# A convolution, attention and gated FFN kernel: t1 kept without its channel mean, and one power for two tiles

## The reference

```
x = inv(I - circulant(ricker(width, damp))) @ x        # over channels
t = tokens(x)
t = t + attention(ln(t))          # 8 heads of 16; linear: elu(q)+1, elu(k)+1, causal sums, divided by the sum of weights; then W_out
u = ln(t)                         # called z in the kernel
g = mean over positions of (relu(u @ gfc1.T + b) @ gfc2.T + b)     # 8 gates for each batch
W1m, b1m, W2m, b2m = base weights + sum over 8 experts of g * expert weights   # for each batch
res = u + relu(u @ W1m.T + b1m) @ W2m.T + b2m
out = t + ln(res) * gain + bias
```

## Time and profile before

| | |
|---|---|
| median of three runs | 734.12 us |
| the profiled execution | 735.35 us |
| its span, first to last instruction | 733.4 us |
| TensorE busy (weight loads, which overlap) | 683.1 us (531.0) |
| DVE, ACT, POOL busy | 647.6, 634.2, 498.8 us |
| first phase | from 16.5 us, steady from about 43 to 448 us, drained at 479.6 us |
| second phase | 479.9 to 733.4 us |

### The profile page before, as it was taken

The page is one execution under the profiler, slowest core; times in us unless marked ns, Lnnn a source line. Parts: engine busy times, 40 slices in busy tenths (PEclk is TensorE's granted clock), DMA queues, the critical chain, the costliest instruction groups (busy, mean ns, idle before and its releaser), DMA issues. The chain is left out here.

```text
span 733.4 us, 39983 instructions
## 1 busy us (share of the span) xinstructions
PE 683.1 (93%) x13026; PEld 531.0 (72%) x13026; DVE 647.6 (88%) x2535; ACT 634.2 (86%) x1780; POOL 498.8 (68%) x911
## 2 busy tenths in 40 slices
PE   3898999999999999999999998889999998999993
PEld 2576777777777777777777776767777797777772
DVE  5689999999999999999999999667998977998983
ACT  3689999999999999999999998457888876888883
POOL 3669999999999999999999997301333312333333
PEclk9999999999999999999999999799999999999998
DMA  4547876666666666666666665210222211222222
GB/s 138 109 111 130 154 139 151 143 147 147 148 138 156 143 144 149 147 152 144 143 149 151 136 142 119 38 37 17 77 83 72 86 44 45 87 72 72 86 86 72
DMA packets 200294, 82.58 MB, mean 113 GB/s; under 512 B 174028, under 2 KB 187503, under 8 KB 200184
## 3 DMA queue, kind: packets, MB, share of 16 engines
q1 hardware_dynamic: 200248, 81.98, 47.7%
HBM read 22.69 MB, written 17.30 MB: 55 GB/s over the span
## 5 line engine op out<-in xcount | busy, mean ns | idle before, releaser
L900 DVE SCALAR_TENSOR_TENSOR scores_lo<-p_a,scores_hi 128x512 f16<-128x512 f32 x256 | 170.6, 677 | 1.2 <-ACT scores_hi L781 1.2
L781 ACT ACTIVATE scores_hi<-p_a 128x512 f16<-128x512 f32 x256 | 162.7, 646 | 4.9 <-PE p_a L617 4.8
L1433 POOL TENSOR_TENSOR ffn_rstd_shift<-ffn_rstd_shift,consts 128x4 f32<-128x4 f32 x32 | 36.8, 1150 | 110.9 <-DVE ffn_rstd_shift L1391 110.9
L1260 ACT ACTIVATE h_f<-psb,merged_b_of_batch 128x512 f32<-128x512 f32 x128 | 87.3, 712 | 11.7 <-PE psb L1196 10.1
L1215 PE MATMUL psb<-merged_W_of_batch,h_hi 128*128 128x128 f16 x512 | 94.5, 220 | 2.3 <-DVE h_lo L1369 1.6
L1369 DVE TENSOR_TENSOR h_lo<-h_f,h_hi 128x512 f16<-128x512 f32 x128 | 95.5, 785 | 1.3 <-ACT h_hi L1271 1.2
L1216 PE MATMUL psb<-merged_W_of_batch,h_hi 128*128 128x128 f16 x512 | 94.2, 220 | 0.0
L1217 PE MATMUL psb<-merged_W_of_batch,h_lo 128*128 128x128 f16 x512 | 94.2, 220 | 0.0
L634 PE MATMUL p_o<-v_parts,scores_hi 128*128 128x17 f16 x1024 | 90.4, 171 | 2.4 <-issue 0.6
L1001 POOL CAST qk_parts<-qk_f 128x512 f16<-128x512 f32 x128 | 78.3, 612 | 17.9 <-issue 15.7
L634 PEld LDWEIGHTS p_o<-v_parts,scores_hi 128*128 128x128 f16 x1024 | 81.6, 96 | 11.8 <-issue 9.2
(11 more groups left out here) (214 smaller groups left out, 2775.3 us busy)
## 6 DMA issues: line engine op xcount, KB each, us to landing
x_f<-in_x SPq DMA_DIRECT2D x32, 256.0 KB, 3.0
t_rows<-t SPq DMA_DIRECT2D x64, 128.0 KB, 2.0
t_back<-t_rows SPq DMA_DIRECT2D x32, 256.0 KB, 2.6
out<-out_tile SPq DMA_DIRECT2D x32, 256.0 KB, 2.0
tv_share<-in_L_ffn_tv_W SPq DMA_DIRECT2D x32, 128.0 KB, 2.2
qkT_parts<-qk_parts SPq DMA_TRANSPOSE x128, 3.1
zT_hi_lo<-z_parts SPq DMA_TRANSPOSE x64, 2.4
merged_W<-in_L_ffn_W SPq DMA_DIRECT2D x2, 256.0 KB, 4.3
```

What stands on the lines that cost most here:

```text
L781: nc.scalar.activation(ah[:, t % 2, cols], p_a[:, cols], ACT.Relu).then_inc(ahi_ready[eo], 1)
L900: nc.vector.scalar_tensor_tensor(al[:, t % 2, cols], p_a[:, cols], 0.0, ah[:, t % 2, cols], ALU.max, ALU.subtract).then_inc(alo_ready[eo], 1)
L1260: nc.scalar.activation(hf_[:, c, :], ps[:, c, :], ACT.Relu, bias=b1s[:, h // 2, c:c + 1], scale=1.0 / WS).then_inc(h_ready[c], 1)
```

## The change

t1 is made without its mean over channels. The inverse's part of `out_project` is now taken from the centred inverse, W_out is centred too, and a column with the mean is put beside them, so that the matmuls have 129 columns; the setup makes these columns. `yt`, its rows in DRAM and `t1_back` are 129 wide. z then needs no bias: `shift2` is gone, and `normalise` is a copy with a scale. `eps2` and `rsqrt2` handle two tiles at once, at the second of them; for this z and all behind it (`normalise`, `z_hi`, `z_lo`, `turn_z`, `gate`, `gate_relu`) stand two slots later, and `stats2` has eight buffers in place of four. In the second phase a new operation on POOL, `add_mean`, adds the mean back to the loaded t1, and `add_up` waits for it in place of the load.

```diff
+C1 = C + 1
+Q0 = C + 16
-TENSOR_ORDER = [("gate", 14), ...
+TENSOR_ORDER = [("gate", 16), ...
-SCALAR_ORDER = [("v_hi", 2), ("normalise", 10), ...
+SCALAR_ORDER = [("v_hi", 2), ("normalise", 12), ...
...
-FFN_GPSIMD_ORDER = [("rsqrt", 2), ("gain", 2)]
+FFN_GPSIMD_ORDER = [("add_mean", 2), ("rsqrt", 2), ("gain", 2)]
...
-                    nc.vector.tensor_scalar(wbig[:, 0:C], pa[:, 1, 0:128], WSI, None, ALU.mult)
+                    nc.vector.tensor_scalar(wbig[:, 0:C], pa[:, 1, 128:256], WSI, None, ALU.mult)
+                    link(nc.vector.tensor_reduce(wom[:, 2:3], pa[:, 1, 0:128], AX.X, ALU.add))
+                    nc.vector.tensor_scalar(wbig[:, C:Q0], wom[:, 2:3].broadcast_to([P, Q0 - C]), WSI / C, None, ALU.mult)
                     link(nc.vector.tensor_copy(gfh[:, :], wsqT[:, 4, :]))
                     dve.wait_ge(s_wtc, 1)
-                    nc.vector.tensor_scalar(woT[:, :], wsqT[:, 3, :], WSI, None, ALU.mult)
+                    link(nc.vector.tensor_reduce(wom[:, 0:1], wsqT[:, 3, :], AX.X, ALU.add))
+                    link(nc.vector.tensor_scalar(wom[:, 1:2], wom[:, 0:1], 1.0 / C, None, ALU.mult))
+                    nc.vector.tensor_scalar(woT[:, 0:C], wsqT[:, 3, :], wom[:, 1:2], WSI, ALU.subtract, ALU.mult)
+                    nc.vector.tensor_scalar(woT[:, C:C1], wom[:, 1:2], WSI, None, ALU.mult)
...
-                        o, cols = p_m1[:, 0:P], slice(j * P, (j + 1) * P)
-                        mm(o, xh[:, hf, cols], wh[:, 0:C], start=True, stop=False)
+                        o, cols = p_m1[:, 0:C1], slice(j * P, (j + 1) * P)
+                        mm(o, xh[:, hf, cols], wh[:, 0:C1], start=True, stop=False)
...
-                        nc.scalar.activation(yt[:, t, :], p_m1[:, 0:P], ACT.Copy, scale=1.0 / WSI).then_inc(t1_ready, 1)
+                        nc.scalar.activation(yt[:, t, :], p_m1[:, 0:C1], ACT.Copy, scale=1.0 / WSI).then_inc(t1_ready, 1)
...
                     def normalise(b, t):
                         n = TILES * b + t
-                        act.wait_ge(shift_ready, n + 1)
+                        act.wait_ge(rstd2, n + 1)
                         at_least(act, zlo_ready, n - 1)
-                        nc.scalar.activation(z_[:, t % 2, :], yt[:, t, :], ACT.Identity, bias=st2[:, t % 4, 10:11],
-                                             scale=st2[:, t % 4, 8:9]).then_inc(z_ready, 1)
+                        nc.scalar.activation(z_[:, t % 2, :], yt[:, t, 0:C], ACT.Copy, scale=st2[:, t, 8:9])\
+                            .then_inc(z_ready, 1)
...
                     def eps2(b, t):
+                        if t % 2 == 0:
+                            return
                         n = TILES * b + t
                         dve.wait_ge(mv2, n + 1)
-                        nc.vector.tensor_scalar(st2[:, t % 4, 9:10], st2[:, t % 4, 7:8], EPS, None, ALU.add)\
-                            .then_inc(ve2, 1)
+                        nc.vector.tensor_scalar(st2[:, t - 1:t + 1, 9:10], st2[:, t - 1:t + 1, 7:8], EPS, None, ALU.add)\
+                            .then_inc(ve2, 2)
...
-                    def shift2(b, t):
-                        n = TILES * b + t
-                        dve.wait_ge(rstd2, n + 1)
-                        nc.vector.tensor_scalar(st2[:, t % 4, 10:11], st2[:, t % 4, 6:7], -1.0, st2[:, t % 4, 8:9],
-                                                ALU.mult, ALU.mult).then_inc(shift_ready, 1)
...
                     def rsqrt2(b, t):
-                        n = TILES * b + t
-                        s = st2[:, t % 4, :]
+                        if t % 2 == 0:
+                            return
+                        n = TILES * b + t
                         pool.wait_ge(ve2, n + 1)
-                        nc.gpsimd.tensor_tensor(s[:, 8:9], s[:, 9:10], mhalf, ALU.pow).then_inc(rstd2, 1)
+                        nc.gpsimd.tensor_tensor(st2[:, t - 1:t + 1, 8:9], st2[:, t - 1:t + 1, 9:10],
+                                                kcol("mhalf")[:, 0:2].unsqueeze(2), ALU.pow).then_inc(rstd2, 2)
...
-                        dve.wait_ge(t1_loaded[hf], 16 * (2 * pair + h // 2 + 1))
-                        nc.vector.tensor_tensor(rn[:, hf, :, :], rn[:, hf, :, :], t1b[:, hf, :, :], ALU.add)\
+                        dve.wait_ge(raised, q + 1)
+                        nc.vector.tensor_tensor(rn[:, hf, :, :], rn[:, hf, :, :], t1b[:, hf, :, 0:C], ALU.add)\
                             .then_inc(v_ready, 1)
...
+                    def add_mean(g, pair, h):
+                        q, hf = HB * pair + h, h % 2
+                        pool.wait_ge(t1_loaded[hf], 16 * (2 * pair + h // 2 + 1))
+                        nc.gpsimd.tensor_tensor(t1b[:, hf, :, 0:C], t1b[:, hf, :, 0:C],
+                                                t1b[:, hf, :, C:C1].broadcast_to([P, HALF, C]), ALU.add)\
+                            .then_inc(raised, 1)
```

More of the change, by code:

```diff
@@ L39 @@
 BIG = -1.0e30
-TENSOR_ORDER = [("gate", 14), ("project", 1), ("state", 3), ("scores", 4), ("turn_out", 6), ("conv", 0),
+TENSOR_ORDER = [("gate", 16), ("project", 1), ("state", 3), ("scores", 4), ("turn_out", 6), ("conv", 0),
                 ("values", 5), ("out_project", 6)]
-SCALAR_ORDER = [("v_hi", 2), ("normalise", 10), ("split_x", 0), ("tv_hi", 0), ("relu_qk", 2), ("gate_relu", 14),
+SCALAR_ORDER = [("v_hi", 2), ("normalise", 12), ("split_x", 0), ("tv_hi", 0), ("relu_qk", 2), ("gate_relu", 16),
                 ("read_t1", 7), ("exp_qk", 1), ("state_hi", 3), ("scores_hi_0", 4), ("copy_out", 6),
@@ L48 @@
 VECTOR_ORDER = [("invert", 6), ("stats2", 8), ("divide", 6), ("make_qk", 2), ("v_lo", 2), ("mean_var2", 8),
-                ("state_lo", 3), ("stats1", 0), ("tv_lo", 0), ("eps2", 8), ("shift2", 9), ("mean_var1", 0),
-                ("scores_lo_0", 4), ("eps1", 0), ("scores_lo_1", 4)]
-GPSIMD_ORDER = [("split_x", 0), ("rsqrt2", 9), ("qk_hi", 2), ("z_hi", 10), ("qk_lo", 2), ("z_lo", 10),
+                ("state_lo", 3), ("stats1", 0), ("tv_lo", 0), ("eps2", 8), ("mean_var1", 0), ("scores_lo_0", 4),
+                ("eps1", 0), ("scores_lo_1", 4)]
+GPSIMD_ORDER = [("split_x", 0), ("rsqrt2", 9), ("qk_hi", 2), ("z_hi", 12), ("qk_lo", 2), ("z_lo", 12),
                 ("rsqrt1", 0)]
-SYNC_ORDER = [("turn_z", 12), ("store", 7), ("turn", 2), ("load_x", 3), ("load_tv", 1)]
+SYNC_ORDER = [("turn_z", 14), ("store", 7), ("turn", 2), ("load_x", 3), ("load_tv", 1)]
 FFN_TENSOR_ORDER = [("up_0", 0), ("up_3", 0), ("up_1", 0), ("down_0", 1), ("down_1", 1), ("down_2", 1),
@@ L215, in build @@
             casd = sb(su, "cas_scaled", [P, 2, C])
-            wbig = sb(su, "w_in", [P, 4 * C])
+            wbig = sb(su, "w_in", [P, Q0 + 3 * C])
+            wom = sb(su, "w_out_mean", [P, 3])
             cw = sb(su, "centred_inverse", [P, C])
@@ L965, in _ @@
                     run(dve, VECTOR_ORDER, {"tv_lo": tv_lo, "stats1": stats1, "mean_var1": mean_var1, "v_lo": v_lo,
-                        "make_qk": make_qk, "shift2": shift2, "state_lo": state_lo,
+                        "make_qk": make_qk, "state_lo": state_lo,
                         "scores_lo_0": scores_lo(0), "scores_lo_1": scores_lo(1),
```

46 lines of the change are left out of this document (23 added, 23 removed).

## The result

The changed kernel takes 761.52 us (median of 6 runs, 759.41 to 762.92), the one before 734.63 in the same series: a ratio of 1.0359, 95% interval 1.0332 to 1.0387. The forecast was 766 with a range of 746 to 775, and slower with a chance of 0.84. The profiled execution has a span of 759.13 in place of 733.44.

| stretch | before | after | difference | predicted |
|---|---|---|---|---|
| start to the first `scores_lo` (setup) | 28.73 | 29.64 | +0.91 | +1.0 |
| to the end of the last `scores_lo` (first phase) | 431.28 | 427.63 | -3.65 | -2.2 |
| to the end of the last gate (drain) | 18.88 | 21.63 | +2.75 | +2.6 |
| to the first `gain` | 28.18 | 28.78 | +0.60 | 0 |
| to the end of the last `gain` (second phase) | 221.29 | 246.34 | +25.05 | +30.2 |

The account below looks back on a forecast made before the run. The second phase was taken as bound by a gain-to-gain loop without slack, the first by a four-tile loop across engines; 734.12 + 31.6 (+30.2 second phase, -2.2 first, +2.6 drain, +1.0 setup) gave 766, range 746 to 775.

Parts of the forecast that it names:

- add_mean on the two hidden_lo: Second phase: add_mean runs between the two hidden_lo and makes the second 1.08 later, 28 times, +30.2 us.
- rival 4: Second phase: add_mean waits for one hidden_lo and is slower than gain, giving 776 us; chance 0.06.
- That the loop has no slack and POOL's own time is free: Second phase: gain to gain fills the whole 6.55 period; POOL idles 2.3, so by its time alone add_mean costs nothing.
- Turns alternate: Second phase: DVE and POOL take turns by who waited longer, so add_mean gets in after the first hidden_lo.
- rival 1: Second phase: DVE keeps its turn, add_mean starts after add_up and the power is 0.55 later; 751 us, chance 0.14.
- Casts: Second phase: the cast beside POOL's power was not held up, so nothing was charged for casts.
- First phase: Four-tile loop: +0.20 for the power, -0.09 for normalise, -0.18 for DVE, so -0.07; 32 loops, -2.2 us.
- The pair's power: First phase: rsqrt2 making two columns takes 0.75 for 0.55, +0.20 on the four-tile loop.
- Drain and setup: End of first phase: last z two slots later, +2.6 us; setup: added row sums and small operations on DVE, +1.0.

Follow-up runs that it names:

- no_add: The changed kernel without POOL's add_mean, add_up waiting for the load itself; 733.31 us, ratio 1.0015 to the kernel before.
- power_in_place: The changed kernel with add_mean replaced, at the same place in POOL's queue, by a power of 128x4; ratio 1.0009 to the kernel before.
- early_before: The kernel before the change with mean_var and add_eps of the second phase moved right behind stats on DVE; 724.71 us, ratio 0.9904.
- after_power: The changed kernel with add_mean between the power and gain in POOL's order; 758.03 us, ratio 1.0335 to the kernel before.
- early_after: The changed kernel with mean_var and add_eps right behind stats on DVE and add_mean behind the power on POOL; ratio 0.9939 to the kernel before.
- bias_back: The changed kernel with the first phase's normalise reading a bias column again; ratio 1.0417 to the kernel before.
- two_powers: The changed kernel with the second norm's epsilon and power made for each tile separately, z still two tiles later; ratio 1.0346 to the kernel before.

## Why the prediction was right, point by point

- *add_mean on the two hidden_lo.* Right in mechanism and in order: POOL gets its turn between the two, the first is unchanged, the second waits and then runs its usual 0.55 past the end of the POOL operation. The mis-sized term is add_mean's duration: "the nearest row is `gain` with the same shape, 1.27". It takes 1.04. With that the step gives itself: 1.04 - 0.14 is 0.90, and add_mean ends 0.90 after the first `hidden_lo` (569.88 and 568.98). 1.08 - 0.23 is the measured 0.85, and 28 x 0.85 = 23.8 stands for 30.2. My rival 4, which made add_mean dearer than `gain`, erred to the other side.
- *That the loop has no slack and POOL's own time is free.* Shown by no_add and power_in_place. TensorE was nearer to being a bound than I wrote: with the stall gone the period falls only from 6.59 to 6.38 (early_before), so the loop was 0.21 longer than TensorE's own work.
- *Turns alternate* (against rival 1). That POOL gets in between two DVE operations that follow each other closely is shown by the two records above: had DVE kept its turn, the second `hidden_lo` would have stayed at 0.68 and add_mean's record been 2.9. Whether turns alternate, or simply go to the one that asked first, is not told apart: add_mean starts to wait at 568.39, the second `hidden_lo` at 568.90, and in after_power too the one that was 0.06 ahead went first.
- *Casts.* I charged nothing, since the cast beside the power was not held up. The number came out right, because no cast lies beside add_mean in the changed kernel; that is luck, for the reason was wrong and the row misread. The cast had begun first (563.27, the power at 563.42), so it was the power that had to wait, and it did: it took 1.15, where it takes 1.01 with nothing of DVE beside it (kernel before, near its end). Where the cast begins 0.06 ahead of it, it takes 1.23 (569.98, kernel before), and where the cast begins 0.21 behind it, 1.01 (646.86, changed kernel).

```profile
718.89 1.01 POOL L1433 TENSOR_TENSOR ffn_rstd_shift<-ffn_rstd_shift,consts 128x4 f32<-128x4 f32 x1 [2.32 <-DVE ffn_rstd_shift L1391]
```

  In early_after a cast beside add_mean takes 1.09 for 0.43, and power_in_place shows that a power of four columns does not hold up a `hidden_lo`. The Trainium skill (SBUF — State Buffer, section "Who interferes with whom") counts casts that run in a two-port mode among what contends with GpSimd; early_after agrees.
- *First phase.* The loop over four tiles with one normalise in it is confirmed to the hundredth by bias_back (-0.09). The pair's power was sized +0.20; two_powers shows its net as +0.09 with the halved epsilon in it. Part of the miss is the row I scaled from: the 1.15 of four columns has 0.14 of waiting for the cast in it; from 1.01 it is 0.15 per further column, and two columns take 0.70 (measured 0.71). What is left I put down to the loss of `shift2`, which no run tried by itself: 26.83 - 0.18 - 26.44 = 0.21 per eight tiles, 0.10 per loop, where I had -0.18 for DVE with both. Together -0.105 per loop and not -0.07. The stretch from first to last `scores_lo` differs by up to 3.7 us between profiles of kernels with the same first phase (426.11 to 429.85 in six of them), so the -3.65 of this pair is told less sharply than the period.
- *Drain and setup.* +2.75 and +0.91 where +2.6 and +1.0 stood. The drain with z at 12 took 19.44 to 21.63 in eight profiles, with z at 10 or 11 17.38 to 18.88 in six, so that a hit within 0.15 is partly luck. That TensorE's clock would be low behind it was not foreseen: 0.60 in this pair of profiles, 1.5 to 2.2 against those in which the clock of the kernel before does not fall.

## What to carry to other kernels

When POOL has idle time, ask what DVE does in it before giving it work: here a POOL operation on 512 elements per partition in SBUF held up each DVE operation with two inputs in SBUF that came while it ran, down to one of four elements per partition, and a cast of 128x512; DVE's statistics from PSUM, their aggregate and a subtraction with one input in PSUM passed beside it, and a POOL power of four columns held up none of them. Price such an addition by the instruction that has to wait for it and by who waits for that one; then look for an order in which the loop has slack there, which here made the kernel before faster and the addition nearly free.

Merging two small operations into one pays only in the slot it leaves; where the merged one falls into the fuller of two alternating slots, it can cost more than the two.
